# Four graph layers in one kernel: stationary operands placed 64 bytes above the moving ones

## What is computed

```python
h = jnp.maximum(_layernorm(x, axis=-1), 0.0)
x = x + _L0_gnn_ref(h, adj, adj, ...)      # attention, 8 heads of 32, static masks and adj
h = jnp.maximum(_layernorm(x, axis=-1), 0.0)
x = x + _L1_gnn_ref(h, adj, ...)           # attention, 4 heads of 64, mask adj
h = jnp.maximum(_layernorm(x, axis=-1), 0.0)
x = x + _L2_gnn_ref(h, adj, ...)           # see below
h = jnp.maximum(_layernorm(x, axis=-1), 0.0)
x = x + _L3_gnn_ref(h, adj, ...)           # 8 heads: cosine links times softmax, then a graph product
```

```python
Wh = jnp.einsum('bni,hoi->bhno', h, W) + bW[None, :, None, :]
e = jnp.einsum('bhno,hop->bhnp', Wh, attn)
scores = jnp.einsum('bhnp,bhmp->bhnm', e, Wh)
A_mat = jnp.tanh(jnp.where(adj[:, None, :, :], scores, 0.0))
hp = jax.nn.relu(jnp.einsum('bhnm,bhmo->bhno', A_mat, Wh))
cat = jnp.transpose(hp, (0, 2, 1, 3)).reshape(hp.shape[0], hp.shape[2], -1)
ha = cat @ A_w.T
hf = h @ fc_w.T
coeff = jax.nn.sigmoid(hf @ g1_w.T + ha @ g2_w.T + gbias)
return hf * coeff + ha * (1.0 - coeff)
```

## The kernel before

| tile | start mod 256 |
|---|---|
| ln_hT_hi, ln_hT_lo, ln_hT, ln_h | 160 |
| square_w_hi, square_w_lo (layers 1 and 3) | 160 |
| l0_w_hi, l0_w_lo; l2_g_w_hi, l2_g_w_lo | 224 |
| l0_oT_hi, l0_oT_lo; constants_sb; l2_gT | 128 |
| l1_oT_hi, l1_oT_lo; q and k_bd of layers 0, 1 and 3 | 0 |
| l2_aw_hi, l2_aw_lo, l2_sq_hi, l2_sq_lo | 32 |
| l2_cat, l2_hf, l2_ha, l2_c_diag (hi and lo), l2_a_bd | 160 |
| l2_wh_w_hi / l2_wh_w_lo (rows of 4112 bytes) | 224 / 0 |
| l2_wh (rows of 4112 bytes) | 128 and 144 |
| same_batch | 192 |
| x_res, y, l3_t | 128 |
| l2_gate, l2_diff, l2_part | 160 |

## Time and profile before

### The profile page before, as it was taken

The page is one execution under the profiler, slowest core; times in us unless marked ns, Lnnn a source line. Parts: engine busy times, 40 slices in busy tenths (PEclk is TensorE's granted clock), DMA queues, the critical chain, the costliest instruction groups (busy, mean ns, idle before and its releaser), DMA issues. The chain is left out here.

```text
span 2135.0 us, 52810 instructions
## 1 busy us (share of the span) xinstructions
PE 2034.9 (95%) x18428; PEld 1882.9 (88%) x18428; DVE 1514.9 (71%) x3344; ACT 1001.2 (47%) x2057; POOL 566.6 (27%) x624
## 2 busy tenths in 40 slices
PE   7999999899999799999999999999998899999997
PEld 6888888899998699999999999999998778887886
DVE  7899999677777455555555555555554799999997
ACT  6667666455555322232222232233222567666765
POOL 4344444222222011101111111111111444444442
PEclk9999999999999899999999999999999999999999
DMA  3222222432323200011111111001110122112211
GB/s 104 69 75 70 66 75 75 148 90 82 89 77 90 73 16 26 22 30 30 30 30 30 30 30 30 21 24 30 30 30 21 42 61 60 51 55 60 60 45 45
DMA packets 149370, 113.31 MB, mean 53 GB/s; under 512 B 42944, under 2 KB 148800, under 8 KB 149312
## 3 DMA queue, kind: packets, MB, share of 16 engines
q1 hardware_dynamic: 149312, 112.52, 18.2%
HBM read 78.93 MB, written 33.55 MB: 53 GB/s over the span
## 5 line engine op out<-in xcount | busy, mean ns | idle before, releaser
L273 POOL TENSOR_TENSOR ln_rstd<-ln_var_eps,minus_half 128x2 f32<-128x2 f32 x128 | 90.8, 709 | 904.6 <-DVE ln_var_eps L266 904.6
L1693 ACT ACTIVATE l_cat_hi<-banks 128x512 fp32r<-128x512 f32 x128 | 76.5, 597 | 261.6 <-PE banks L1866 261.6
L161 PE MATMUL banks<-ln_hT_hi,square_w_hi 128*128 128x256 f32 x512 | 155.5, 304 | 5.0 <-DVE square_w_lo L638 3.2
L161 PE MATMUL banks<-ln_hT_hi,l_g_w_hi 128*128 128x256 f32 x512 | 148.6, 290 | 4.9 <-POOL l_a_bd L1646 4.9
L290 ACT ACTIVATE ln_h<-ln_x,ln_shift,ln_rstd 128x256 f32<-128x256 f32 x256 | 139.5, 592 | 28.7 <-DVE ln_shift L280 23.7
L163 PE MATMUL banks<-ln_hT_hi,square_w_lo 128*128 128x256 f32 x512 | 146.2, 285 | 0.0
L162 PE MATMUL banks<-ln_hT_lo,square_w_hi 128*128 128x256 f32 x512 | 146.1, 285 | 0.0
L161 PE MATMUL banks<-l_cat_hi,l_aw_hi 128*128 128x256 f32 x512 | 144.2, 282 | 1.4 <-DVE l_cat_lo L1753 1.4
L163 PE MATMUL banks<-l_cat_hi,l_aw_lo 128*128 128x256 f32 x512 | 144.1, 281 | 0.0
L162 PE MATMUL banks<-l_cat_lo,l_aw_hi 128*128 128x256 f32 x512 | 143.8, 281 | 0.0
L163 PE MATMUL banks<-ln_hT_hi,l_g_w_lo 128*128 128x256 f32 x512 | 142.8, 279 | 0.0
(11 more groups left out here) (234 smaller groups left out, 6984.6 us busy)
## 6 DMA issues: line engine op xcount, KB each, us to landing
hidden<-y SPq DMA_DIRECT2D x96, 256.0 KB, 2.2
ln_x<-hidden SPq DMA_DIRECT2D x96, 256.0 KB, 2.8
x_res<-hidden SPq DMA_DIRECT2D x96, 256.0 KB, 2.9
ln_x<-x SPq DMA_DIRECT2D x32, 256.0 KB, 2.8
x_res<-x SPq DMA_DIRECT2D x32, 256.0 KB, 3.0
out<-y SPq DMA_DIRECT2D x32, 256.0 KB, 2.2
l_adj_u<-adj SPq DMA_DIRECT2D x96, 16.0 KB, 2.4
l_stage_attnT<-L_attnT SPq DMA_DIRECT2D x4, 256.0 KB, 3.2
```

The costliest lines, as they stand in the source:

```text
L161: nc.tensor.matmul(out, lhs(lh), rhs(rh), start=start, stop=False, skip_group_check=True)
L273: self.nc.gpsimd.tensor_tensor(self.rstd[:, g.slot], self.var_eps[:, g.slot], self.core.minus_half[:, 0:PAIRS], ALU.pow).then_inc(self.rst ...
L1693: nc.scalar.activation(cat_hi[:, h * KC:(h + 1) * KC], halves(B_HP[h]), ACT.Relu).then_inc(cat_hi_ready.sem, 1)
```

## The change

A helper `tile` rounds a tile's start up to 256 bytes and adds a pad of 0, 96, 160, 192 or 224 bytes, given per tile; tiles of fewer than 128 elements a partition are made as before. The stationary tiles of fp32 products start at residue 0 and the moving ones at 192. Token tiles in float32r, which are now moving and now stationary, start at 160 (ROWS), weights that are stationary at 224 (HELD_BY_ROWS), weights that move at 96 (MOVED_BY_ROWS). `SquareWeights` has two tiles each for hi and lo where it had one: weights 0 and 1 held, 2 and 3 moved. Tiles that are no operand of TensorE start at 0. The rows of wh_w and wh are 1088 elements apart instead of 1028. THIRDS becomes 320, 384 and 324 columns, so that each block starts at a multiple of 256 bytes. The instructions and their order are otherwise the same.

```diff
+LINE = 256
+BASE = 160
+ROWS = BASE % LINE
+HELD_BY_ROWS = (BASE + 64) % LINE
+MOVED_BY_ROWS = (BASE + 192) % LINE
+HELD, MOVED = 0, 192
...
+def tile(ctx, nc, name, shape, dtype=F32, at=HELD):
+
+    n = math.prod(shape[1:])
+    if n < P:
+        return ctx.enter_context(nc.sbuf_tensor(name, shape, dtype))
+    pad = at // mybir.dt.size(dtype)
+    flat = ctx.enter_context(nc.sbuf_tensor(name, [shape[0], pad + n], dtype, align_bytes=LINE))[:, pad:pad + n]
...
-        self.x_res = ctx.enter_context(nc.sbuf_tensor("x_res", [P, 2, PAIRS, D], F32))
-        self.y = ctx.enter_context(nc.sbuf_tensor("y", [P, 2, PAIRS, D], F32))
+        self.x_res = tile(ctx, nc, "x_res", [P, 2, PAIRS, D], F32)
+        self.y = tile(ctx, nc, "y", [P, 2, PAIRS, D], F32)
...
-        self.hT_hi = sb("hT_hi", [P, 2, KC, TOK], F32R)
-        self.hT_lo = sb("hT_lo", [P, 2, KC, TOK], F32R)
+        self.hT_hi = sb("hT_hi", [P, 2, KC, TOK], F32R, ROWS)
+        self.hT_lo = sb("hT_lo", [P, 2, KC, TOK], F32R, ROWS)
...
-        self.hi = sb("w_hi", [P, 4, KC, D], F32R)
-        self.lo = sb("w_lo", [P, 4, KC, D], F32R)
+        held = [sb(n, [P, 2, KC, D], F32R, HELD_BY_ROWS) for n in ("w_hi_held", "w_lo_held")]
+        moved = [sb(n, [P, 2, KC, D], F32R, MOVED_BY_ROWS) for n in ("w_hi_moved", "w_lo_moved")]
+        self.hi, self.lo = [[held[i][:, 0], held[i][:, 1], moved[i][:, 0], moved[i][:, 1]] for i in range(2)]
...
-        k_bd = sb("k_bd", [P, 2, KC, NB, HPC, S])
-        v_bd = sb("v_bd", [P, 2, PAIRS, 2, HH, 2, VW])
+        k_bd = sb("k_bd", [P, 2, KC, NB, HPC, S], F32, MOVED)
+        v_bd = sb("v_bd", [P, 2, PAIRS, 2, HH, 2, VW], F32, HELD if direct else MOVED)
...
-        probT = sb("probT", [P, 2, NT, TP * HH, P])
+        probT = sb("probT", [P, 2, NT, TP * HH, P], F32, MOVED if direct else HELD)
...
-        oT_hi = sb("oT_hi", [P, 2, KC, TOK], F32R)
+        oT_hi = sb("oT_hi", [P, 2, KC, TOK], F32R, ROWS)
...
-    c = ctx.enter_context(nc.sbuf_tensor("constants_sb", [P, n], F32))
+    c = tile(ctx, nc, "constants_sb", [P, n], F32, MOVED)
...
-        self.g_w_hi, self.g_w_lo = sb("g_w_hi", [P, H, KC, D], F32R), sb("g_w_lo", [P, H, KC, D], F32R)
-        self.wh_w_hi, self.wh_w_lo = sb("wh_w_hi", [P, KC, WC], F32R), sb("wh_w_lo", [P, KC, WC], F32R)
-        self.aw_hi, self.aw_lo = sb("aw_hi", [P, CH, D], F32R), sb("aw_lo", [P, CH, D], F32R)
-        self.sq_hi, self.sq_lo = sb("sq_hi", [P, 3, KC, D], F32R), sb("sq_lo", [P, 3, KC, D], F32R)
+        self.g_w_hi, self.g_w_lo = [sb(n, [P, H, KC, D], F32R, HELD_BY_ROWS) for n in ("g_w_hi", "g_w_lo")]
+        self.wh_w_hi, self.wh_w_lo = [sb(n, [P, KC, PITCH], F32R, MOVED_BY_ROWS)[:, :, 0:WC] for n in ("wh_w_hi", "wh_w_lo")]
+        self.aw_hi, self.aw_lo = [sb(n, [P, CH, D], F32R, HELD_BY_ROWS) for n in ("aw_hi", "aw_lo")]
+        self.sq_hi, self.sq_lo = [sb(n, [P, 3, KC, D], F32R, HELD_BY_ROWS) for n in ("sq_hi", "sq_lo")]
...
-    THIRDS = ((0, 344), (344, 344), (688, WC - 688))
+    THIRDS = ((0, 320), (320, 384), (704, WC - 704))
...
-        gT = sb("gT", [P, H, KC, TOK])
-        wh = sb("wh", [P, PAIRS, WC])
+        gT = sb("gT", [P, H, KC, TOK], F32, MOVED)
+        wh = sb("wh", [P, PAIRS, H * D + S])[:, :, 0:WC]
...
-        a_bd = sb("a_bd", [P, PAIRS, H, 2, S])
-        cat_hi, cat_lo = sb("cat_hi", [P, CH, TOK], F32R), sb("cat_lo", [P, CH, TOK], F32R)
+        a_bd = sb("a_bd", [P, PAIRS, H, 2, S], F32, MOVED)
+        cat_hi, cat_lo = [sb(n, [P, CH, TOK], F32R, ROWS) for n in ("cat_hi", "cat_lo")]
```

More of the change, by code:

```diff
@@ L1 @@
 from contextlib import ExitStack
+import math
 import numpy as np
@@ L25 @@
 LN_EPS = 1e-5
+LINE = 256
[4 more added lines that the diff above has]
+HELD, MOVED = 0, 192
 GROUPS = 32
 AHEAD = 2
+def tile(ctx, nc, name, shape, dtype=F32, at=HELD):
[4 more added lines that the diff above has]
+    flat = ctx.enter_context(nc.sbuf_tensor(name, [shape[0], pad + n], dtype, align_bytes=LINE))[:, pad:pad + n]
+    names = "abcdefg"[:len(shape) - 1]
+    if len(names) == 1:
+        return flat
+    return flat.rearrange(f"p ({' '.join(names)}) -> p {' '.join(names)}", **dict(zip(names, shape[1:])))
 class Signal:
@@ L170, in __init__ @@
         nc = core.nc
-        sb = lambda n, shape, dt=F32: ctx.enter_context(nc.sbuf_tensor(f"ln_{n}", shape, dt))
+        sb = lambda n, shape, dt=F32, at=HELD: tile(ctx, nc, f"ln_{n}", shape, dt, at)
         self.core, self.nc = core, nc
@@ L371, in attention_layer @@
     with ctx:
-        sb = lambda n, shape, dt=F32: ctx.enter_context(nc.sbuf_tensor(f"{tag}_{n}", shape, dt))
+        sb = lambda n, shape, dt=F32, at=HELD: tile(ctx, nc, f"{tag}_{n}", shape, dt, at)
         w_stage, w_hi, w_lo = weights.raw, weights.hi, weights.lo
@@ L957, in place_constants @@
     same_batch = c[:, 2 * P:3 * P]
-    core.same_batch = ctx.enter_context(nc.sbuf_tensor("same_batch", [P, P], F32R))
+    core.same_batch = tile(ctx, nc, "same_batch", [P, P], F32R)
     core.waits_passed = core.once("waits_passed")
@@ L983, in __init__ @@
         self.core, self.square, self.w, self.b = core, square, w, b
-        sb = lambda n, shape, dt=F32: ctx.enter_context(core.nc.sbuf_tensor(f"l3_{n}", shape, dt))
+        sb = lambda n, shape, dt=F32, at=HELD: tile(ctx, core.nc, f"l3_{n}", shape, dt, at)
         self.block_w = sb("block_w", [P, P])
@@ L1066, in gated_graph_layer @@
     with ctx:
-        sb = lambda n, shape, dt=F32: ctx.enter_context(nc.sbuf_tensor(f"l3_{n}", shape, dt))
+        sb = lambda n, shape, dt=F32, at=HELD: tile(ctx, nc, f"l3_{n}", shape, dt, at)
         w_hi, w_lo = weights.square.hi, weights.square.lo
@@ L1537, in __init__ @@
         self.stage = ctx.enter_context(ExitStack())
-        sb = lambda n, shape, dt=F32: self.stage.enter_context(nc.sbuf_tensor(f"l2_stage_{n}", shape, dt))
+        sb = lambda n, shape, dt=F32, at=HELD: tile(self.stage, nc, f"l2_stage_{n}", shape, dt, at)
         self.wb = sb("wb", [P, CH, D + 1])
@@ L1565, in graph_attention_layer @@
     with ctx:
-        sb = lambda n, shape, dt=F32: ctx.enter_context(nc.sbuf_tensor(f"l2_{n}", shape, dt))
+        sb = lambda n, shape, dt=F32, at=HELD: tile(ctx, nc, f"l2_{n}", shape, dt, at)
         weights.stage.close()
@@ L1964, in graph_attention_setup @@
     with ExitStack() as ctx:
-        sb = lambda n, shape, dt=F32: ctx.enter_context(nc.sbuf_tensor(f"l2_stage_{n}", shape, dt))
+        sb = lambda n, shape, dt=F32, at=HELD: tile(ctx, nc, f"l2_stage_{n}", shape, dt, at)
         wh_w = sb("wh_w", [P, KC, HD])
```

41 lines of the change are left out of this document (21 added, 20 removed).

## The result

The changed kernel takes **2123.03 us** (median of 4 runs, 2121.06 to 2124.22) against 2136.36 for the kernel before beside it (4 runs, 2135.16 to 2137.15): ratio 0.9937, 95% interval 0.992 to 0.9954. It is faster by 13.3 us, not by 31.2, and lies above the range of 2092 to 2119. The profiled execution took 2123.79 us with a span of 2121.9.

What follows compares the result with a forecast made beforehand. TensorE was taken to bound layers 1 and 2, VectorE layers 0 and 3. Gains of 15.0 + 6.9 + 5.7 + 2.6 + 1.0 = 31.2 us from 2136.92 gave 2105.7, or 2105.3 us against the median; range 2092 to 2119.

Steps and rivals of the forecast that it cites:

- The rival that TensorE matters there: Layers 0 and 3: all 12.6 us come where 1 is counted, time 2093.7; chance 0.10.
- bystander: Rival for all moved tiles: placement does nothing, the offset being incidental to the 113.3 ns; time 2136.5, chance 0.04.
- the rival of stationary weights alone: +64 works only with weights stationary; layer 1's V and O (3.7 us) and wide blocks (5.7) gain nothing: 2114.7, chance 0.10.
- The slower rival: VectorE in layers 0 and 3 loses 26 ns an instruction by the new placement, 48 us; time 2154, chance 0.03.
- I take 113.3 for 118.8, 5.5 ns for each matmul moved to +64: 256-column matmuls of layers 1 and 2: start to start drops by 5.5 ns each, giving 6.9 and 15.0 us.
- three left out at each entry: Blocks entered behind fp32 work: three matmuls per entry get no gain, one entry in layer 2, three in layer 1.
- aw's 48 and hf's 12: Layer 2: these matmuls per group move to +64 and gain 5.5 ns each, 264 and 66 ns a group.
- The wide blocks: Layer 2, 36 matmuls per group: 320 and 384 columns gain at +64, 324 does not; 5.7 us, bounds 0 and 7.8.
- hp: Layer 2, fp32, 128 columns, 1024 passes: gains 2.7 ns each, down to the transposes' pace; 2.6 us, bounds 0 and 2.6.
- c_diag: Layer 2, four 256-column matmuls per group move to +64 and gain 5.5 ns each, 22 ns a group.
- Layer 1: 48 matmuls per group move to +64, 39 counted after three fp32 entries (Q, K, O); 6.9 us.
- The gate: Layer 2, 24 matmuls per group behind transposes move to +64: 116 ns a group gained, without a wait for ha_lo.

Runs made afterwards that it cites:

- e7: Changed kernel with the square weights of layers 0, 1 and 3 at 160, so their products run at offset 0 instead of +64; 2128.04 us.
- e3: Changed kernel with only layer 2's g weights moved from offset +64 to 128 bytes above their base; 2128.33 us.
- e13: Changed kernel with the second and third wide block of each pair swapped (320, 324, 384 columns), all tiles at the same places; 2112.86 us.
- e6: Changed kernel with the wide blocks' old widths (344, 344, 340) and old weight places restored, the rest as changed; 2115.98 us.
- e14: Changed kernel with two of layer 2's four fp32 transposes moved ahead of aw, the other two left behind hf; 2126.15 us.
- e4: Changed kernel with wide blocks of 256, 260 and 512 columns instead of 320, 384 and 324; 2120.12 us.

## Why the prediction was wrong

**The bound was read rightly.** TensorE's matmuls set layers 1 and 2, VectorE layers 0 and 3. Layer 3 kept its period (14.346 us a group in both), and layer 0 has 11.26 us at +64 and 11.24 at offset 0 (e7). The rival that TensorE matters there is out. In layer 3 the cheaper matmuls went into TensorE's waits; over the whole execution the one for l_linked is 25.6 us against 23.9.

**The offset works, in both roles.** e3 and e7 turn it off, and 113.3 ns becomes 118.9 and 120, so it is no bystander; V, with weights moving, gains 50 ns a group, so the rival of stationary weights alone is out as well.

**VectorE lost nothing.** Its y in layer 3 takes 715 ns, l_part 692, ha_lo 0.69 us, as in the earlier trace rows. The slower rival has no part in it.

**The step that failed is "I take 113.3 for 118.8, 5.5 ns for each matmul moved to +64", with three left out at each entry.** It took the pace of the earlier trace rows for the pace of the offset. There are two at +64, and aw's 48 and hf's 12, 60 of layer 2's 88 moved matmuls of 256 columns, landed on 117.8 in nearly all groups: gained 62 and 17 ns a group where 264 and 66 were counted, 251 ns or 8.0 us over 32 groups. e13 and e6 give them the fast pace with aw's and hf's own offset unchanged and find that much: a group of layer 2 is 0.233 and 0.224 us shorter, 7.5 and 7.2 us in all., g's first intervals at 120 in front of 113, was read as a start that always passes; it doesn't. The earlier trace rows misled further: 118.5 ns for aw at +128 lies so near the middle pace, 117.8, that a row at one pace does not tell what +64 would give.

**The wide blocks**, 5.7 us counted, brought 0.3 (8 ns a group). The low bound, from the earlier trace rows, was the measured truth: one wide pair at +64 had shown no gain. I set it aside because it stood alone, and carried the 6.6 ns over from 256 columns by a rule of whole multiples of 256 bytes that no row showed. With its effect on aw the part costs some 6 us (e6).

**hp**, 2.6 us counted, brought nothing (3404 and 3405 ns a group). Its difference of 3 ns from the transposes is not one of offset.

**c_diag**'s four matmuls, 0.7 us counted, brought nothing (562 and 564 ns). They follow the gate with nothing between; its last ones run at 113 ns, they at 117 to 119. I had counted this border as no entry at all; why the pace isn't kept there stays open.

**Layer 1**, 6.9 us counted, gave 3.2 by the layers' spans. Q gained its 47 ns. K's went into a wait for l_prob, which I had not looked for: I checked what could be late next in layer 2 only. O and V are fast in 22 and 23 of 32 groups here, in 24 to 31 in the other profiles of the same layout; in the best of them (e14) layer 1 took 2.7 us less.

**The gate** was sized rightly, 97 of 116 ns, ha_lo was no wait, and the transposes stood as they were (four of ln_h take 356 and 357 ns, four of l_yT 355 and 353, medians), so nothing was lost at fp32.

Sum: layer 2 18.2 us short, layer 1 3.7, against 2.0 more in layer 0, 1.5 in the set-up and 0.3 at the start, together 18.1 of the 31.2. The range failed with it: its low end still gave every 256-column matmul 113.3 in the end, and wide and hp at nothing took only 8.3 us off. That the kernel would be faster, given 0.93, came true.

## What to carry over

A pace read in one block is evidence for that block; before it is multiplied over others, look for the same operation at the same setting in a second place with other neighbours, and bound the sum by the case that the new blocks don't reach it. When a stretch gets a few per cent cheaper, look at every hand-over inside it, not only at the longest one. And after moving tiles, compare one matmul tile by tile, by its median and from start to start: a reordering that changes no address was worth another 8 us here.

## What the hardware showed that I had not expected

- 256-column fp32r matmuls, each with a new weight load, run at 113.3 or 117.8 ns at +64 (276 or 281 ns as the profile draws one), and at 118 to 120 at the other offsets of these kernels. Which of the two it is holds for a whole block and hangs on the matmuls before it; with their order alone changed, aw went from 4 fast blocks of 32 to 31.
- At other widths no offset tried helped: 320 to 384 columns cost 12 to 14 ns above their columns at 2.4 GHz at +64, and up to 19 at the others; 260 columns (120 ns) cost as much as 256 off +64, and 512 cost 22 ns above theirs.
- The Trainium skill ("TensorE: Matmul & The Clock Gate", Back-to-back issue gap) gives 109.2 ns for 256 columns by its formula, which it calls the gap of an isolated matmul; the prediction left that word out. For a stream with weight loads it states some 131 ns at 512 columns. Neither fits fp32r here: in none of the sixteen traces has a block of 256 columns, each matmul with a weight load, a median below 113, and 512 columns took 235 (e4).
